# Bias of 78 main pairs added by VectorE in PSUM, and 80 instead of 74 main pairs among the message pairs

## What is computed

```python
hx = einsum('ni,rio->rno', x, weight)            # x: 50000 x 256, weight: 8 x 256 x 256
msg = hx[edge_type, src]                         # 12500 edges
agg = segment_sum(msg, dst, 50000)               # dst is sorted
node = agg * C + h_bias + (x @ loop_weight) * C
out = layernorm(x + node)                        # over the 256 columns, without scale and shift
```

## Time and profile before

| | |
|---|---|
| median of 3 runs | 756.22 us (753.68 to 757.34) |
| the profiled execution | 756.98 us, its span 755.3 us |
| TensorE busy | 633.6 us (84%), weight loads 566.6 us (75%) |
| VectorE busy | 553.4 us (73%), 1843 instructions |
| ScalarE busy | 484.2 us (64%) |
| GpSimd busy | 466.0 us (62%) |
| the bias matmul, L1167 | 196 times, 99.3 us busy, 506 ns each |
| `xt_low`, L788 | 221 times, 151.4 us busy, 685 ns each |
| `stats` of main pairs, L795 | 336 instructions, 126.4 us busy |

### The profile page before, as it was taken

The page is one execution under the profiler, slowest core; times in us unless marked ns, Lnnn a source line. Parts: engine busy times, 40 slices in busy tenths (PEclk is TensorE's granted clock), DMA queues, the critical chain, the costliest instruction groups (busy, mean ns, idle before and its releaser), DMA issues. The chain is left out here.

```text
span 755.3 us, 15565 instructions
## 1 busy us (share of the span) xinstructions
PE 633.6 (84%) x4470; PEld 566.6 (75%) x4470; DVE 553.4 (73%) x1843; ACT 484.2 (64%) x1150; POOL 466.0 (62%) x468
## 2 busy tenths in 40 slices
PE   1499999599999998999999999999899888988430
PEld 1378877588888898888989999878787786877310
DVE  4998654776676676767675679989989898889540
ACT  1857875256566666666766567778677777777620
POOL 6980000777777777777775740676776767676273
PEclk9999999799999999999999999999999999999855
DMA  4534455479888888988787589899999999996421
GB/s 146 175 103 131 158 167 169 122 266 335 290 283 300 304 297 307 310 297 289 275 283 223 178 294 291 256 314 319 331 326 297 328 316 331 314 329 211 155 92 41
DMA packets 71393, 187.92 MB, mean 249 GB/s; under 512 B 12890, under 2 KB 28672, under 8 KB 71311
## 3 DMA queue, kind: packets, MB, share of 16 engines
q1 hardware_dynamic: 51727, 139.68, 54.9%
q0 software_dynamic: 19584, 47.23, 19.0%
HBM read 107.60 MB, written 85.59 MB: 256 GB/s over the span
## 5 line engine op out<-in xcount | busy, mean ns | idle before, releaser
L788 DVE TENSOR_TENSOR xt_low<-xt_ps,xt_high 128x512 fp32r<-128x512 f32 x221 | 151.4, 685 | 91.3 <-ACT xt_high L1004 88.6
L1176 PE MATMUL y_ps<-w_high,xt_high 128*128 128x256 f32 x672 | 190.8, 284 | 0.0
L1176 PE MATMUL y_ps<-w_high,xt_low 128*128 128x256 f32 x672 | 190.5, 284 | 0.0
L1176 PE MATMUL y_ps<-w_low,xt_high 128*128 128x256 f32 x672 | 190.4, 283 | 0.0
L562 POOL DMA_INDIRECT gathered<-in_x,src_at x105 | 112.9, 1075 | 110.6 <-DVE edge_at L772 78.9
L1004 ACT ACTIVATE xt_high<-xt_ps 128x512 fp32r<-128x512 f32 x221 | 130.2, 589 | 40.0 <-PE xt_ps L1144 39.3
L591 POOL DMA_INDIRECT out_rows<-y_fix,fix_at x99 | 99.0, 1000 | 73.9 <-ACT y_fix L1076 51.0
L1042 ACT ACTIVATE y_out<-y_ps,rstd 128x256 f32<-128x256 f32 x336 | 138.9, 467 | 3.4 <-DVE rstd L826 3.2
L1144 PE MATMUL xt_ps<-ident,x_in 128*128 128x128 f32 (+1 forms) x784 | 118.8, 275 | 25.5 <-DMA x_in<-in_x 15.8
L1176 PEld LDWEIGHTS y_ps<-w_high,xt_low 128*128 128x128 f32 x672 | 128.6, 191 | 7.5
L569 POOL DMA_INDIRECT message_rows<-message_out,edge_at x105 | 106.2, 1012 | 43.3 <-issue 28.1
(11 more groups left out here) (166 smaller groups left out, 1069.7 us busy)
## 6 DMA issues: line engine op xcount, KB each, us to landing
x_in<-in_x SPq DMA_DIRECT2D x97, 512.0 KB, 5.1
out_rows<-y_out SPq DMA_DIRECT2D x97, 512.0 KB
message_in<-message_rows SPq DMA_DIRECT2D x99, 128.0 KB
column_of<-out_rows SPq DMA_DIRECT2D x14, 512.0 KB
out_rows<-column_of SPq DMA_DIRECT2D x14, 512.0 KB, 3.9
keys<-key_table SPq DMA_DIRECT2D x12, 512.0 KB, 6.4
w_rel<-in_L_gnn_weight SPq DMA_DIRECT2D x1, 2048.0 KB, 13.5
gathered<-in_x,src_at POOLq DMA_INDIRECT x105, 4.5
```

What stands on the lines that cost most here:

```text
L788: nc.vector.tensor_tensor(xt_low[:, q % XT_RING, :], xt_ps[q % 2][:, :], xt_high[:, q % XT_RING, :].bitcast(F32), ALU.subtract).then_inc(l ...
L1176: return nc.tensor.matmul(to, xt[:, at_row:at_row + P], w, start=start, stop=stop)
```

## The change

The main pairs that stand between the first and the last message pair (there are 72 of them with `MIXED` = 74, and 78 with 80) no longer get their bias by the matmul of L1167. In its place VectorE adds the bias to the finished product in the PSUM bank, one instruction over 128 x 512, before the pair's statistics are taken. In VectorE's order it stands before `low(s + 2)`. `MIXED` goes from 74 to 80, so that six main pairs (three blocks) that had a fix beside them now stand among the message pairs.

```diff
-MIXED = 74
+MIXED = 80
...
+        BIAS_BY_DVE = [n for n in sorted(m_at) if g_at[0] < m_at[n] < g_at[MPAIRS - 1]]
+        bias_number = {n: i + 1 for i, n in enumerate(BIAS_BY_DVE)}
...
+            def add_bias(m):
+                if m not in bias_number:
+                    return
+                dve.wait_ge(product, m_at[m] + 1)
+                y = y_ps[bank[m_at[m]]][:, :].rearrange("p (t d) -> p t d", t=2)
+                nc.vector.tensor_tensor(y, y, bias_b[:, :].unsqueeze(1).broadcast_to([P, 2, D]), ALU.add).then_inc(biased, 1)
+
             def take_stats(m):
                 b = m // 2
                 wait(dve, moments, b - 3 - HELD)
-                dve.wait_ge(product, m_at[m] + 1)
+                if m in bias_number:
+                    dve.wait_ge(biased, bias_number[m])
+                else:
+                    dve.wait_ge(product, m_at[m] + 1)
...
+                if kind_before == "m" and s > HOLD:
+                    add_bias(before)
                 low(s + 2)
                 if kind_before == "m" and s > HOLD:
                     take_stats(before)
...
-                if kind == "m":
+                alone = kind == "g" or n in bias_number
+                if not alone:
                     nc.tensor.matmul(y_ps[bank[q]][:, :], ones_r[:, :], bias_rows[:, :], start=True, stop=False)
...
-                        first, end = kind == "g" and k == 0, k == KT - 1 and (kind == "g" or t == 1)
+                        first, end = alone and k == 0, k == KT - 1 and (alone or t == 1)
```

More of the change, by code:

```diff
@@ L343, in gnn_layernorm_kernel @@
         masks_built = sem("masks_built")
+        biased = sem("biased")
         edge_key_ready = sem("edge_key_ready")
@@ L1156, in multiply @@
             def multiply(q, offsets):
-                kind = slots[q][0]
+                kind, n, _ = slots[q]
                 held = q < HOLD
```

## The result

The changed kernel takes 778.87 us (778.44 to 780.01), the kernel before beside it 755.75: a ratio of 1.031, 95% interval 1.028 to 1.034. Slower was forecast, 765; it is 23 us and not 9, and above the range's end of 777.

What follows compares the result with a forecast made beforehand. TensorE was taken to bound the message stage, with GpSimd and the VectorE-ScalarE loop close behind. From 757.0, +19 us there and -11 among the fixes gave 765; range 748 to 777.

Steps and rivals of the forecast that it cites:

- TensorE sets the pace, two others close behind: Message stage before: TensorE's 276.3 of 280.1 us sets its end; GpSimd's DMAs (277.2) and the VectorE-ScalarE loop follow closely.
- TensorE's gain of 24 us is lost: Message stage: dropping 78 bias products at 0.31 us saves TensorE 24 us, but the VectorE-ScalarE loop takes its place.
- The 17 us that the prediction set aside: TensorE's gain by the Trainium skill's 216 ns per 512-column matmul; the prediction used the row's 0.31 us instead.
- The add at 0.61, bounds 0.34 to 0.79: VectorE's bias add in PSUM: 0.61 us to the next instruction, taken from `low`; 47.6 us for 78 adds.
- One add of two is on the loop: VectorE-ScalarE loop: a block's first add falls in idle time, its second is exposed; the loop grows 0.61 us, not 1.22.
- Three more blocks and held blocks, message stage 299: Message stage with six more main pairs and 14 held blocks prolonging the loop: 299 us, +19.
- The loop's sum of 263: VectorE-ScalarE loop over the message stage before the change: 20 x 5.80 + 16 x 7.6 + 25 = 263 us.
- The other two routes: Message stage after: block sums of 309 less up to 10 give 300 to 305; 280.1 less 24.2, plus 24 and 12, 292.
- Six pairs fewer beside the fixes, -11: Fixes' stage: six fewer main pairs save 12.3 us by VectorE or 10.3 by DMA; -11 taken, range -8 to -13.
- Rival D: Message stage: the add costs 0.79 us through a PSUM write or semaphore, +7 to +14, total 772 to 779; chance 0.21.
- B: Message stage: VectorE's adds stay hidden, GpSimd's pace of 277 us is the floor, total 743; chance 0.18.
- C: Message stage: the loop's 24 us of air absorbs the adds, three more blocks cost +12, total 757; chance 0.15.

Runs made afterwards that it cites:

- first74: Changed kernel with 74 main pairs among the messages, VectorE adding only each block's first-pair bias, TensorE the second: ratio 0.999 to the kernel before, message stage 277.1 us.
- dve74: Changed kernel with `MIXED` = 74, VectorE adding the bias of both pairs of a block: message stage 285.2 us; the bias alone is +3 us.
- pe80: Kernel before with `MIXED` = 80, every bias still on TensorE: 772.29 us against 758.22.

## Why the prediction was right or wrong

- *TensorE sets the pace, two others close behind.* Right only in that three limits lay close together; which came first was misread. The prediction's own sums were 276.3 for TensorE and 277.2 for GpSimd, and GpSimd ran without a pause in 40 of 51 steps. The 26.6 us ahead of message pairs' products were counted as TensorE's work; they grew to 33.3 in `first74` and 47.7 in the changed kernel as TensorE had less to do, so at least a part of them was room.
- *TensorE's gain of 24 us is lost.* Lost it is, but it was 78 x 0.24 = 19 us: a main pair takes 1.87 without its bias, not 1.80. The 17 us that the prediction set aside were nearer. With the adds of first pairs alone 3.0 us of the gain show (277.1), with the others none.
- *The add at 0.61, bounds 0.34 to 0.79.* Right: 0.59 to the next instruction (423.43 to 424.02), 0.68 long. The sentence of the Trainium skill weighed there ("VectorE: DVE Perf Modes", "The DRAIN you can't avoid"), that the next operation waits for the pipe to empty, would give 0.68 or more if taken alone; the same section adds that a next operation that is not held starts earlier. The trace agrees with the addition: the next instruction starts 0.09 before the recorded end.
- *One add of two is on the loop.* Right, and shown by itself: 277.1 against 284.6.
- *Three more blocks and held blocks, message stage 299.* Right: 298.0. The loop's sum of 263 with 36 adds of 0.61 gives 285, and `dve74` measured 285.2; with 39 adds and 12 us for the blocks it gives 299. The other two routes gave 292 and 300 to 305, and 299 was picked between them, so that 1 us of error is partly luck. The term for the six pairs alone, 12 us, measured 12.8 with VectorE's bias (285.2 to 298.0) and 8.0 with TensorE's.
- *Six pairs fewer beside the fixes, -11.* Wrong, and this is the whole miss: +4 in place of -11 is 15 us, and 14 are missing (778.9 against 765). The failed step reads: "GpSimd, two DMAs for each of the 99 fixes, allows it: it waited 50.4 - 25.9 = 24.5 us for `y_fix` in 21 places behind the first". I let VectorE's work and the DMA share set the pace (-12.3 and -10.3 us for six pairs) and took a wait of the last engine in the chain for room. It was the mark of a loop, just as I had read it in the message stage ("long waits on both sides with neither busy"), and the other half of the mark was there: VectorE's 8.7 us for the gathered rows, a row that I did not use. The prediction's signs of being wrong did name fixes that gain under 8 us because GpSimd holds them, but with no price or chance. With more room on the way (gathers three groups ahead) six pairs are worth 7.6 to 9.1 us; with the late norms too 7.7 (233.2 to 225.5). So even then the term was too large by 2 to 3.4 us. Why the stage grew by 4 us (8 in `pe80`), and did not just stay, is in part argued: longer slots on the way fit the rows.
- *Rival D* named a dearer add for 772 to 779. The time came out there, but not for this reason: the add was 0.59. B and C are out by the message stage's 298.
- *The range* had no case in which the fixes' stage doesn't gain: its term went from -8 to -13 only.

## What to carry to other kernels

Work put on an engine that is not full (VectorE was busy for 190 of 280 us here) costs what it adds to the loop it stands in, so find the instruction that waits behind it, and count only that. Of two like instructions one can be free and the other wholly exposed. Where a stage has waits on two engines for each other's product, one round a DMA included, look for the number of periods that the way may take before you count on taking work out: work that isn't on the way buys nothing, and if the way holds a fixed number of steps, fewer and longer steps can make it worse (here likely, not settled). And measure the whole program, not the stage alone: of the 17 us that the longer lead took off one stage, 5 came back behind it.

## What the runs showed of the hardware

VectorE adding 128x512 in place in a PSUM bank, with a row of SBUF read for both halves, takes 0.68 us, and 0.59 from its start to the next instruction: as much as a subtraction that writes SBUF (0.69 and 0.60 to 0.61). I had kept 0.79 open. TensorE's 512-column product of the bias starts 0.31 us before the next matmul, but without it a main pair is only 0.24 us shorter (2.11 to 1.87). GpSimd issues an indirect DMA of 128 rows every 1.33 us when nothing holds it (four in 5.33, among the messages), and a group of eight among the fixes in 10.5.
